# A four-layer graph network: one-hot matrices that hold y, kept in DRAM for two later edge passes, and node work inside the edge passes

## The reference

```python
edge_index = jnp.stack([src, dst])
h = jnp.maximum(_layernorm(x, axis=-1), 0.0)
x = x + _L0_gnn_ref(h, node_vec1, edge_attr_4, edge_attr_8, ...)
h = jnp.maximum(_layernorm(x, axis=-1), 0.0)
x = x + _L1_gnn_ref(h, node_vec1, edge_attr_4, edge_attr_8, ...)
h = jnp.maximum(_layernorm(x, axis=-1), 0.0)
x = x + _L2_gnn_ref(h, edge_attr_16, edge_attr_4, ..., edge_index)
h = jnp.maximum(_layernorm(x, axis=-1), 0.0)
x = x + _L3_gnn_ref(h, node_vec1, node_vec1_n2, node_vec1_n3, edge_attr_4, edge_attr_10, src, dst, ...)
```

```python
h = jax.nn.silu(edge_scalars @ fcW1 * (1.0 / np.sqrt(RAD)))
w = h @ fcW2 * (1.0 / np.sqrt(HID))
wA, wB, wC, wD = (w[:, :64], w[:, 64:128], w[:, 128:160], w[:, 160:192])
xs, xv = f_s[edge_src], f_v[edge_src]          # rows of the source nodes
y0, y1 = edge_attr[:, :1], edge_attr[:, 1:4]
outA = wA * xs * y0
outD = wD * jnp.einsum('eud,ed->eu', xv, y1) * INV3
outB = wB[:, :, None] * xs[:, :, None] * y1[:, None, :]
outC = wC[:, :, None] * xv * y0[:, :, None]
agg = jax.ops.segment_sum(edge_feat, edge_dst, num_segments=n)
...
return cos * sc + sin * conv
```

## Time and profile before

| | us |
|---|---|
| three runs: lowest, median, highest | 7206.0, 7221.93, 7224.54 |
| profiled execution, span | 7226.5 |
| PE busy, share of the span | 6569.0, 91% |
| PEld busy | 5175.8, 72% |
| DVE busy | 4888.2, 68% |
| ACT busy | 3087.1, 43% |
| POOL busy | 4427.4, 61% |

### The profile page before, as it was taken

The page is one execution under the profiler, slowest core; times in us unless marked ns, Lnnn a source line. Parts: engine busy times, 40 slices in busy tenths (PEclk is TensorE's granted clock), DMA queues, the critical chain, the costliest instruction groups (busy, mean ns, idle before and its releaser), DMA issues. The chain is left out here.

```text
span 7226.5 us, 182541 instructions
## 1 busy us (share of the span) xinstructions
PE 6569.0 (91%) x51671; PEld 5175.8 (72%) x51671; DVE 4888.2 (68%) x14416; ACT 3087.1 (43%) x8581; POOL 4427.4 (61%) x3934
## 2 busy tenths in 40 slices
PE   6999999799999857999999999999947879999998
PEld 3777778576666736878878777787836744777777
DVE  4666665476666545777777777777657975666665
ACT  2444443333333344666666666666530012333332
POOL 1777773277777216888877887878720011777772
PEclk9999997599999756889898888989778955999996
DMA  1222221222222213444444444444426701222221
GB/s 61 68 68 68 68 68 34 58 68 68 69 69 68 44 60 61 83 82 83 82 81 80 82 81 81 82 80 83 78 52 174 200 5 36 69 69 69 69 69 44
DMA packets 730807, 526.10 MB, mean 73 GB/s; under 512 B 244683, under 2 KB 677819, under 8 KB 730083
## 3 DMA queue, kind: packets, MB, share of 16 engines
q0 software_dynamic: 263424, 321.38, 22.1%
q1 hardware_dynamic: 467300, 203.73, 11.0%
HBM read 429.13 MB, written 95.55 MB: 73 GB/s over the span
## 5 line engine op out<-in xcount | busy, mean ns | idle before, releaser
L606 POOL DMA_INDIRECT l_edge_g<-node_table,l_edge_idx x2352 | 2281.7, 970 | 1124.3 <-issue 702.9
L649 PEld LDWEIGHTS l_edge_win_ps<-l_edge_hot,l_edge_prod 128*32 128x32 f32 (+2 forms) x23520 | 1515.3, 128 | 247.7 <-issue 170.4
L649 PE MATMUL l_edge_win_ps<-l_edge_hot,l_edge_prod 128*32 128x40 f32 (+2 forms) x23520 | 1620.9, 227 | 4.3 <-DVE sums_T L732 4.3
L1121 POOL DMA_INDIRECT att_g<-node_table,att_ends x784 | 1250.4, 1595 | 238.9 <-issue 238.6
L672 ACT ACTIVATE l_edge_gy<-l_edge_g,y 128x160 f32<-128x160 f32 x2352 | 811.7, 416 | 791.9 <-DMA l_edge_g<-node_table,l_edge_idx 789.3
L1114 POOL DMA_INDIRECT att_g<-node_table,att_ends x784 | 792.8, 1011 | 415.2 <-issue 281.3
L636 PE MATMUL l_edge_w_ps<-l_edge_wo,l_edge_h 128*128 128x384 f32 (+1 forms) x3136 | 907.1, 423 | 0.2 <-ACT l_edge_h L664 0.2
L664 ACT ACTIVATE l_edge_h<-l_edge_h_ps 128x256 f32<-128x256 f32 (+1 forms) x784 | 337.8, 431 | 1126.3 <-PE l_edge_h_ps L624 1076.6
L1141 PE MATMUL att_turn<-ident,sums_T 128*128 128x128 f32 (+1 forms) x4704 | 775.0, 309 | 30.1 <-ACT sums_T L1226 23.7
L636 PEld LDWEIGHTS l_edge_w_ps<-l_edge_wo,l_edge_h 128*128 128x128 f32 (+1 forms) x3136 | 536.8, 191 | 336.1 <-issue 171.7
L1226 ACT ACTIVATE sums_T<-att_turn 128x512 f32<-128x512 f32 (+1 forms) x1176 | 665.3, 591 | 216.7 <-PE att_turn L1141 211.8
(11 more groups left out here) (232 smaller groups left out, 11533.8 us busy)
## 6 DMA issues: line engine op xcount, KB each, us to landing
l_messages<-att_rows SPq DMA_DIRECT2D x196, 320.0 KB
sum_msg<-l_messages SPq DMA_DIRECT2D x196, 320.0 KB, 3.6
l_edge_g<-node_table,l_edge_idx POOLq DMA_INDIRECT x2352
att_g<-node_table,att_ends POOLq DMA_INDIRECT x1568
node_table<-l_rows SPq DMA_DIRECT2D x245, 80.0 KB, 1.6
att_ea<-in_edge_attr_T SPq DMA_DIRECT2D x196, 64.0 KB
l_scores<-att_score SPq DMA_DIRECT2D x784, 2.0 KB
l_edge_idx<-in_src_groups SPq DMA_DIRECT2D x588, 2.0 KB, 1.7
```

What stands on the lines that cost most here:

```text
L606: pool.indirect_dma_start(g[s][:, t, :], None, rows_of, bass.IndirectOffsetOnAxis(idx[s][:, t:t + 1], 0)).then_inc(fetched[s], 16)
L649: ins = nc.tensor.matmul(at, q[:, t, lo:lo + width], to[:, t, kinds, :], start=t == 0, stop=t == TG - 1)
L1121: pool.indirect_dma_start(g[s1][:, t, :], None, table[3], bass.IndirectOffsetOnAxis(ends[s1][:, TG + t:TG + t + 1], 0), compute_op=ALU.add ...
```

## The change

All of y goes into the one-hot matrices: four kinds (y0 and the three of y1) of 128 edges x 40 nodes for each of the four tiles, 128 x 640 numbers or 320 KB a group. The l0 pass makes them and SP stores them to a table in DRAM; l1 and l3 load them. The products are then plain ones of w and gathered rows (three operations on DVE), gy is gone, and 24 matmuls instead of 20 make the window sums. For l0 and l1 the w matmuls take 64 rows and 192 columns, alternating between the upper and lower half of the rows.

The same function, `edge_stream`, also takes in the post pass and the next layer's node pass: a tail (`TailL0`, `TailL1`, `TailL3`) works on node tile t as soon as its groups are summed, one tile per four groups, with small steps put behind those of the edge groups on each engine. `post_l0`, `post_l1`, `post_l3`, the node passes l1 and l2 and `store_x` are no longer run on this path (the node pass l3 is). The weights of a tail are loaded at the fifth step. A loop of 36 steps is written out before the repeated part. After setup and the l0 node pass, the widest window is read and a branch picks the new path (`streamed`) or the old functions under the names `any_` (`general`). The diff's core, with lines that are alike left out:

```diff
+        def edge_stream(tag, rows_of, edge_T, w_in, w_mid, w_out, act_fn, scales, tail, turns_behind):
+            K = 4
+            U = 4
+            FETCH = 4
+            WARM = 36
+            lag = 2
+            after = TG * turns_behind
+            makes_hot = tag == "l0"
...
+                    @block.sync
+                        def step(i, s, r):
+                            if live(i, NG):
+                                at_least(sp, fetched[s], 16 * TG * r)
+                                sp.dma_start(idx[s][:, :], A["src_groups"][ds(i * P, P), :]).then_inc(idx_loaded[s], 16)
+                                at_least(sp, hidden[0], i - 1)
+                                sp.dma_start(ea[s % 2][:, :], A[edge_T][:, ds(i * HC, HC)]).then_inc(ea_loaded[s % 2], 16)
+                                if not makes_hot:
+                                    at_least(sp, summed, i - H + 1)
+                                    sp.dma_start(hot[s][:, :, :, :].rearrange("p t k n -> p (t k n)"), hot_tiles[ds(i * P, P), :]
+                                                 ).then_inc(hot_moved[s], 16)
+                            if makes_hot and live(i - 3, NG):
+                                s3, _ = back(s, r, 3, U)
+                                at_least(sp, made, (i - 3) * K + 2)
+                                sp.dma_start(hot_tiles[ds((i - 3) * P, P), :], hot[s3][:, :, :, :].rearrange("p t k n -> p (t k n)")
+                                             ).then_inc(hot_moved[s3], 16)
+                            if isinstance(i, int) and i == 4:
+                                own.sp_load(sp)
+                            own.sp(sp, i, s, r)
...
+                    @block.gpsimd
+                        def step(i, s, r):
+                            own.pool(pool, i, s, r)
+                            if live(i, NG):
+                                gate(pool, (w_loaded, W_LOAD),
+                                     (idx_loaded[s], 16 * (r + 1)),
+                                     (made, (i - 3) * K))
+                                for t in range(TG):
+                                    pool.indirect_dma_start(g[s][:, t, :], None, rows_of,
+                                                            bass.IndirectOffsetOnAxis(idx[s][:, t:t + 1], 0)).then_inc(fetched[s], 16)
...
+                    @block.tensor
...
+                                for n in range(TG // HALVES):
+                                    for m in range(HALVES):
+                                        ins = nc.tensor.matmul(w_ps[s1][:, m * (TG // HALVES) + n, 0:wn],
+                                                               h[last][s1][m * hid:(m + 1) * hid, n * P:(n + 1) * P],
+                                                               wo[m * hid:(m + 1) * hid, :])
+                                ins.then_inc(weighed, 1)
...
+                                sums = [(win[:, 0:W], S0, P, slice(0, 1)), (win[0:SC, W:(1 + XYZ) * W], S1, SC, slice(1, 1 + XYZ)),
+                                        (win[SC:MID, W:2 * W], V0 + 2 * VC, VC, slice(0, 1))]
+                                for at, lo, width, kinds in sums:
+                                    for t in range(TG):
+                                        nc.tensor.matmul(at, q[:, t, lo:lo + width], to[:, t, kinds, :], start=t == 0, stop=t == TG - 1)
+                                for c in range(XYZ):
+                                    lo = V3 + c * VC
+                                    for t in range(TG):
+                                        ins = nc.tensor.matmul(win[SC:MID, 2 * W:3 * W], q[:, t, lo:lo + VC], to[:, t, 1 + c, :],
+                                                               start=c + t == 0, stop=c + t == XYZ + TG - 2)
+                                ins.then_inc(summed, 1)
+                            own.pe(pe, i, s, r)
...
+                                nc.vector.tensor_tensor(to[:, :, :, :], here[:, :, :].unsqueeze(2).to_broadcast([P, TG, 1 + XYZ, EDGE_WIN]),
+                                                        y.to_broadcast([P, TG, 1 + XYZ, EDGE_WIN]), ALU.mult).then_inc(made, 1)
...
+            def post_sums(self, pe, t, whole, vectors, last):
+                at_least(pe, self.gathered, t + 1)
+                nc.tensor.matmul(whole, self.sums[:, 0, :], self.w0[:, :], start=True, stop=False)
+                nc.tensor.matmul(vectors, self.sums[0:MID, 1, :], self.w1[0:MID, :], start=False, stop=False)
+                nc.tensor.matmul(whole, self.sums[0:MID, 2, :], self.w2[0:MID, :], start=False, stop=False)
+                nc.tensor.matmul(last, self.sums[0:SC, 3, :], self.top[0:SC, :], start=False, stop=True).then_inc(self.posted, 1)
...
+        class TailL0(NodeTail):
...
+            def pe(self, pe, i, s, r):
+                if (t := tile_of(i, s, r, 3, 4)) is not None:
+                    self.map(pe, t)
+                if (t := tile_of(i, s, r, 1, 3)) is not None:
+                    at_least(pe, self.done, t * self.KD)
+                    self.post(pe, t)
+                if (t := tile_of(i, s, r, 1, 4)) is not None:
+                    self.turn(pe, t, 1)
...
+            def pool(self, pool, i, s, r):
+                if (t := tile_of(i, s, r, 0, 4)) is not None:
+                    at_least(pool, self.done, (t + 1) * self.KD)
+                    at_least(pool, self.tile_ready, t)
+                    stream_scale(pool, self.settled, t, self.mv, self.half[:, 0:1], self.scales[:, 0:1], self.scales[:, 1:2], self.rooted)
```

More of the change, by code:

```diff
@@ L32 @@
 EDGE_WIN, SUM_WIN = 40, 64
+SLACK = 2
 COLS = NPAD + SUM_WIN
@@ L122, in all_windows @@
         sums("", True)
-        widest = nc.values_load(span[0:1, 0:1], min_val=0, max_val=NODES)
         with nc.If(widest >= width):
@@ L158, in setup @@
                 span_f = sbuf(ctx, "span_f", [1, 2 * NG + 1])
+                tile_end = sbuf(ctx, "tile_end", [1, NT - 1], I32)
+                late = sbuf(ctx, "late", [1, NT])
                 ones_row = sbuf(ctx, "ones_row", [1, P])
@@ L183, in _ @@
                         nc.gpsimd.iota(diag_i[:, :], pattern=[[1, P]], base=0, channel_multiplier=-1).then_inc(iotas, 1)
+                        nc.gpsimd.iota(tile_end[:, :], pattern=[[P, NT - 1]], base=P, channel_multiplier=0).then_inc(iotas, 1)
                     @block.vector
@@ L574, in edge_pass @@
                 last = layers - 1
-                W_LOAD = 16 * HALVES * len(maps)
+                W_LOAD = 16 * HALVES * (len(blocks) + 1)
                 def half(s, r):
@@ L584, in _ @@
                     def _(sp):
-                        sp.wait_ge(w_zeroed, len(maps))
-                        for w, name in maps:
+                        sp.wait_ge(w_zeroed, len(blocks))
+                        for w, name in blocks:
                             rows, cols = A[name].shape
@@ L589, in _ @@
                                 sp.dma_start(w[n * rows:(n + 1) * rows, n * cols:(n + 1) * cols], A[name]).then_inc(w_loaded, 16)
+                        for n in range(HALVES):
+                            sp.dma_start(wo[n * hid:(n + 1) * hid, :], A[w_out]).then_inc(w_loaded, 16)
                         def step(i, s, r):
@@ L679, in _ @@
                     def _(dve):
-                        for w, _ in maps:
+                        for w, _ in blocks:
                             nc.vector.memset(w[:, :], 0.0).then_inc(w_zeroed, 1)
@@ L733, in add_window, with stream_stats, stream_scale @@
                                     ALU.add).then_inc(added, 1)
+        def stream_stats(dve, settled, k, row, stat, mv, done):
+            gate(dve, settled, (done, k))
+            nc.vector.bn_stats(stat[:, :], row).then_inc(done, 1)
+            gate(dve, settled, (done, k + 1))
+            nc.vector.bn_aggr(mv[:, :], stat[:, :]).then_inc(done, 1)
+            dve.wait_ge(done, k + 2)
+            nc.vector.tensor_scalar(mv[:, 1:2], mv[:, 1:2], EPS, None, ALU.add).then_inc(done, 1)
+        def stream_scale(pool, settled, t, mv, half, scale, bias, rooted):
+            nc.gpsimd.tensor_tensor(scale, mv[:, 1:2], half, ALU.pow).then_inc(rooted, 1)
+            gate(pool, settled, (rooted, 2 * t + 1))
+            nc.gpsimd.tensor_scalar(bias, mv[:, 0:1], scale, -1.0, ALU.mult, ALU.mult).then_inc(rooted, 1)
@@ L1748, in build @@
                   [(0, SC ** -0.5), (0, VC ** -0.5)])
[L1749 to L1765 removed]
+        clear_sems(0, len(layer_sems))
+        nc.all_engine_barrier()
+        widest = nc.values_load(span[0:1, 0:1], min_val=0, max_val=NODES)
+        with nc.If(widest < EDGE_WIN):
+            streamed()
+            clear_sems(0, len(layer_sems))
+        with nc.Else():
+            side[0] = "any_"
+            general()
+            clear_sems(0, len(layer_sems))
 def kernel(**inputs):
@@ L1806 @@
     a = padded(given.pop("edge_attr_8"), EPAD)
-    arrays["edge_attr_8_T"] = a.reshape(NG, TG // 2, 2, P, -1).transpose(2, 4, 0, 1, 3).reshape(2 * a.shape[1], -1)
```

(1 more changed line is left out.)

619 lines of the change are left out of this document (583 added, 36 removed).

## The result

| | before | changed |
|---|---|---|
| runs: lowest, median, highest | 7205.25, 7213.97, 7224.54 | 7136.07, 7144.93, 7151.63 |
| profiled execution, span | 7226.5 | 7132.6 |
| mean granted clock | 0.872 | 0.901 |

The account below looks back on a forecast made before the run. PE and POOL were taken as full in the edge passes. Passes +421, new loads and branch +18, joins -538: -99 on the profiled 7226.5, so 7127.5; forecast 7123 us after allowing for the median, range 6910 to 7320.

Parts of the forecast that it names:

- w: Message weights on PE in l0 and l1: 64-row matmuls in pairs take 0.70 us, -0.5 us a group in l0.
- the window sums: Window sums on PE in the edge passes: wider and more matmuls add 0.53 us a group, between +0.32 and +0.6.
- The tail of l0: Post, transposes, map and shape changes on PE: 2.55 us a tile, +0.64 us a group in l0 and l1.
- the joins: Between passes and at the end of l3: 48, 72 and 30 us remain, with the result's store spread, saving 538 us.
- the middle: Attention, softmax, sums and l3 node pass between l1 and l3: same code in both kernels, counted as equal.
- the pause: At each edge pass's start, DVE stands at its fifth step for the tail's weight loads: 5 us each, 15 in all.
- point 5: Tails' small operations on POOL between gathers: 0.48 us each, +0.48 us a group in l1.
- rival B: POOL: small operations at 1.25 us each give 7274, at 1.0 no change; longer gathers would do the same; chance 0.12.
- Rival A: In l0 and l1 the halves of w don't overlap on PE: 1.25 us, 7323 in all; chance 0.12.
- Rival E: Halves of w overlap, but two changes of matmul shape cost 0.16 us each: 0.32 a group, 7233; chance 0.05.
- C: Added PE passes cost half: 0.58 us less a group in l0, 0.5 in l3, -212, 6911 us; chance 0.12.
- D: A window is too wide, so the run-time branch runs the old passes: 7225 us, no change; chance 0.03.

Follow-up runs that it names:

- e_w_one_half: The changed kernel with all four w matmuls of a group in l0 and l1 reading rows 0-63 (wrong values, same amount of work): 7411.3 us.
- e_w_serial: The changed kernel with the w matmuls in l0 and l1 issued rows 0-63 twice, then rows 64-127 twice: 9592.9 us, ratio 1.0206 to the kernel before.

## Why the prediction was right, and where it was off

The direction and the account behind it hold, with one term mis-sized; the size holds in the profiled executions (-94 us for -99) and less well by the medians (-69).

- *PE in l0 and l3.* A group of l0 without tail was put at 5.14 us and is 5.15, from two misses that cancel: w is 0.85, not 0.70 (-0.34 instead of -0.5), and the window sums add 0.38, not 0.53 (2.98 to 3.36). In l3 they add 0.48; a group is 5.57 for 5.64. The tail of l0 is 2.59 a tile for 2.55, the post of l3 1.96 for 1.9.
- *The total is closer than its parts, and that is luck.* Against the forecast l1 is 49 us longer and l0 6; l3 is 25 shorter, the joins 9, the middle 15. The middle, which was to stay equal, hides a third of the miss in l1. In l3 a group without tail is 0.07 us shorter than forecast (14 us), and the pause of 5 did not come.
- *The step that was mis-sized* is point 5. A small operation was priced at the iota's 0.18 and one gap; the power takes 0.58 us (128x2: 0.74), the multiplication 0.26, the second waits 0.17 for the first, and the gather behind has a gap of 0.55 instead of 0.30. That makes 0.68 us a group, not 0.48: 40 us of l1, by POOL's rows. That is rival B's mechanism at about a quarter of its price (40 of 151 us). Its other half, gathers made longer by the added transfers, did not come.
- *The pause* was put at 5 us a pass; it is 16 in l0 and some 18 in l1, since SP issues the loads only when its own fifth step comes and DVE stands for 9.4 us.
- *Joins*: -547 for -538. The tails of the last tiles fit into 41 and 65 us. What the work costs where it went: in the join of l0 and l1 PE was busy for 198 us at clock 0.53, the half clock of the forecast (0.53 in the other join, 0.57 at the end), most of it with this work, and the tails of l0 take it 2.59 x 49 = 127 us at 0.99.
- *The middle* was counted as equal and is 15 us shorter, all of it and a little more in the attention (2562.0 to 2542.4); not explained.
- Rival A of the chances is that the halves of w don't overlap: 1.25 us for L920, 0.55 a group more than the 0.70 of the forecast, 108 us in l0, 92 in l1 and 7323 in all. It did not come, and e_w_one_half gives its price: +145 and +133. In l0 the eight passes cost 0.64 us a group more, not 0.55, which is 125 us, and the clock there is 0.97 instead of 0.99; in l1 it is 0.91 instead of 0.93. Rival E is that they overlap but that each of the two changes between the 64-row matmuls and the others costs the late start of 0.16 us of the earlier trace rows: 0.32 a group, 7233 in all. It came in part: the load behind the 64-row passes starts 0.23 us late, which is why w is 0.85; the load before them has the same gap of 0.33 that followed L913's counterpart in the kernel before. What makes these gaps no run shows. C and D did not come.

The net of 1% is the difference of two numbers near 500, and it was seen only where the mean granted clock is 0.9. On a chip at 0.74 a kernel with the changed kernel's work, e_w_serial, was 2.1% slower than the kernel before (ratio 1.0206, 1.0162 to 1.0250), and so was each of the other seven runs at that clock, by 1.5% or more; the forecast had no rival for this.

## What to carry to other kernels

Work that ran alone in a join here, at a clock of 0.53, cost PE less inside a pass at 0.99 (most of 198 us there, 127 in l0), but it then counts at the pass's bound, whichever engine that is: price it per group and per engine. Look for the smallest engine operation ahead of a saturated queue; here two GpSimd instructions on 128x1 cost as much of POOL's time (1.30 us) as one gather of 128 rows (1.25). A gain that rests on one engine's clock should be measured on more than one chip.
